# A third row block of attention probabilities is transposed through DRAM, with its spreads, PSUM banks and one reload moved

## What is computed

```python
qu, ku, vu, qc, kc, vc = split(xn @ W_qkv.T)            # each [b, 8 heads, 512, 64]
term1     = where(j > i, 0, qc*s @ vu.T)
lookahead = where(j > i, sigmoid(qu*s @ ku.T), 0)
Su        = term1 @ lookahead.T                          # [b, h, 512, 512]
scores    = qc*s @ kc.T - silu(Su);  masked where j > i
out       = softmax(scores) @ vc
ffn       = (silu(xn @ wg.T) * (xn @ wu.T)) @ wd.T       # hidden size 768, int weights / 127
```

## Time and profile before

| what | value |
|---|---|
| median of 3 runs | 1081.72 us (1080.22 to 1082.07) |
| the profiled execution | 1082.21 us, its span 1080.2 us |
| TensorE busy | 1058.2 us, 98% of the span |
| VectorE busy | 871.9 us, 81% |
| ScalarE busy | 755.8 us, 70% |
| GpSimd busy | 567.1 us, 52% |
| TensorE's granted clock, mean | 0.996 |

### The profile page before, as it was taken

One profiled execution on the slowest core, in us unless ns is written; L12 is line 12 of the kernel. 1 busy time (PEld: TensorE's weight loads), 2 busy tenths in 40 slices (PEclk: granted clock), 3 DMA queues, 4 the chain that ended last, 5 costly groups with the idle time before them and its releaser, 6 DMA issues.

```text
span 1080.2 us, 21562 instructions
## 1 busy us (share of the span) xinstructions
PE 1058.2 (98%) x7652; PEld 947.6 (88%) x7652; DVE 871.9 (81%) x1831; ACT 755.8 (70%) x1483; POOL 567.1 (52%) x630
## 2 busy tenths in 40 slices
PE   6999999999999999999999999999999899999998
PEld 5888888888888888888888889988889888899997
DVE  5788789888988898889888988888777768667766
ACT  6678777877787778777877787778777755443333
POOL 5355565556555655565556555656555545422230
PEclk9999999999999999999999999999999989999999
DMA  5032434343434343344334343433324546556631
GB/s 195 1 79 64 118 89 110 76 104 102 91 96 101 105 101 86 91 116 89 99 77 130 79 109 76 125 79 80 98 59 123 161 144 237 175 179 217 214 133 60
DMA packets 246076, 120.72 MB, mean 112 GB/s; under 512 B 161232, under 2 KB 227024, under 8 KB 243920
## 3 DMA queue, kind: packets, MB, share of 16 engines
q1 hardware_dynamic: 245968, 119.31, 40.5%
HBM read 64.75 MB, written 54.53 MB: 110 GB/s over the span
## 4 chain that ended last, share of the span: by engine, by line
PE 89%; DVE 3%; ACT 2%; issue 2%; POOL 1%; DMA 1%; SPq 1%; DVEq 0%; POOLq 0%; ACTq 0%
PE X L833 23%; PE X L748 20%; PE X L986 7%; PE X L885 7%; PE X L977 7%; PE X L817 6%; PE X L801 5%; PE X L787 5%; PE X L772 4%; PE X L867 4%; POOL prob L668 1%; DMA xT<-xT_copy 1%; DVE L_s L1457 1%; ACT prob L1176 1%; ACT T_s L1154 1%
## 5 line engine op out<-in xcount | busy, mean ns | idle before, releaser
L668 POOL TENSOR_SCALAR prob<-prob,inv 128x512 f32<-128x512 f32 (+3 forms) x256 | 301.4, 1194 | 16.3 <-DVE inv L1499 16.3
L833 PE MATMUL X<-L_s,T_s 128*128 128x128 f32 (+3 forms) x1920 | 281.7, 301 | 2.0 <-DVE L_s L1457 2.0
L833 PEld LDWEIGHTS X<-L_s,T_s 128*128 128x128 f32 x1920 | 267.5, 189 | 13.4 <-issue 2.8
L748 PE MATMUL X<-xT,W 128*128 128x512 f32 (+1 forms) x972 | 244.8, 399 | 0.0
L748 PEld LDWEIGHTS X<-xT,W 128*128 128x128 f32 x972 | 175.7, 191 | 40.8 <-issue 0.4
L1168 ACT ACTIVATE gate<-X 128x1024 f32<-128x1024 f32 (+1 forms) x96 | 84.9, 884 | 154.7 <-PE X L833 154.7
L642 POOL TENSOR_SCALAR_AFFINE_SELECT gate<-gate 128x256 f32<-128x256 f32 (+1 forms) x96 | 47.5, 495 | 205.2 <-DVE gate L1471 205.2
L1471 DVE SCALAR_TENSOR_TENSOR gate<-gate,X 128x1024 f32<-128x1024 f32 (+1 forms) x96 | 99.6, 1038 | 64.0 <-ACT gate L1168 64.0
L658 POOL TENSOR_SCALAR_AFFINE_SELECT T_s<-T_s 128x512 fp32r<-128x512 f32 x128 | 104.6, 829 | 85.4 <-DVE T_s L1464 85.4
L1176 ACT ACTIVATE prob<-prob,least 128x512 f32<-128x512 f32 (+3 forms) x256 | 141.8, 587 | 1.5 <-DVE least L1487 1.5
L1487 DVE CUSTOM_DVE_ANT_0 prob<-X,gate 128x512 f32<-128x512 f32 (+3 forms) x256 | 112.8, 487 | 25.8 <-PE X L817 24.2
(11 more groups left out here) (108 smaller groups left out, 1888.2 us busy)
## 6 DMA issues: line engine op xcount, KB each, us to landing
heads_out<-o_s SPq DMA_DIRECT2D x62, 256.0 KB, 3.3
prob_raw<-prob SPq DMA_DIRECT2D x240, 64.0 KB, 1.9
PT_s<-prob_raw SPq DMA_DIRECT2D x120, 128.0 KB, 2.4
xT_copy<-xT SPq DMA_DIRECT2D x8, 1024.0 KB, 6.8
w_split<-w_parts SPq DMA_DIRECT2D x22, 256.0 KB, 2.5
W<-w_split SPq DMA_DIRECT2D x12, 384.0 KB, 6.9
xT<-xT_copy SPq DMA_DIRECT2D x4, 1024.0 KB, 6.3
tanh_l<-in_L_attn_x SPq DMA_DIRECT2D x8, 512.0 KB, 4.9
```

The lines of the kernel that those rows point to most:

```text
L668: last = pool.tensor_scalar(v, v, inv[:, h, w - 1:w], None, ALU.mult)
L748: last = pe.matmul(out[:, tokens], sh.W[:, a, k, cols], xT[:, c, k, tokens], start=(n == 0), stop=(n == 3 * KD - 1))
L833: last = pe.matmul(both[:, h, at:at + (J + 1) * P], T_s[:, h, a, to:to + P], L_s[:, h, c, WIDE[J + 1]:WIDE[J + 1] + (J + 1) * P], start=(J ...
```

## The change

- Query row block 2 (query rows 256 to 383, three blocks per head) leaves TensorE too. `turn_heads` now transposes three blocks per head, both heads in one go, behind `sum_up` 0; `high_heads` and `low_heads` copy them in two instructions each. Nothing is transposed behind `sum_up` 1.
- `row_in_squares` runs twice on VectorE: row block 3 (128x1024) and, behind low VU, row block 2 (128x768). `prob` is laid out by row block, so that both heads lie side by side and a row block leaves in 4 spreads instead of 8.
- SyncE issues the 4 spreads of row 3 and the 4 of row 2, and only then the loads of row 3 (4) and row 2 (3).
- `high_rows` and `low_rows` work on 128x1536 and 128x256 elements, where `high_last_row` and `low_last_row` worked on 128x768 and 128x256.
- VectorE's low QU and low KU move behind `inverse` 2.
- Banks: `sum_up` 0 goes to banks 2 and 3, `sum_up` 1 to 6 and 7 (they swap), and the products of the last steps follow.
- `load_xT(0)` moves from step 31 to step 30, behind `load_gate_up` and ahead of the spreads; `load_down_out` stays in step 31, with no wait of its own.

The diff, cut to its core:

```diff
-         ("Su", 0, (6, 7)), ("PH", 0, (0, 1)), ("PT", 0, (0, 1)), ("PT", 1, (4,)), ("Su", 1, (2, 3)),
-         ("PH", 1, (6, 7)), ("PT", 2, (6, 7)), ("Su", 2, (4, 5))]
+         ("Su", 0, (2, 3)), ("PH", 0, (0, 1)), ("PT", 0, (0, 1)), ("PT", 1, (4,)), ("Su", 1, (6, 7)),
+          ("PT", 2, (2, 3)), ("Su", 2, (4, 5))]
...
+        def prob_row(h, w):
+            return flat_prob[:, 2 * WIDE[w] + h * w * P:2 * WIDE[w] + (h + 1) * w * P]
...
                 if part == LAST and q == 3:
+                    load_down_out()
+                if part == LAST and q == 2:
+                    load_gate_up()
                     sp.wait_ge(proj_filled, proj_count(LAST_G, KC))
                     sp.wait_ge(v_filled, LAST_G + 1)
                     sp.wait_ge(xT_stored, BATCH * 16)
                     load_xT(0)
-                    load_down_out()
-                if part == LAST and q == 2:
-                    load_gate_up()
                 if back1 and g - 1 < SQUARED:
-                    spread_last_row(g - 1, back2)
+                    for I in (3, 2):
+                        spread_row(g - 1, I)
+                    if back2:
+                        sp.wait_ge(o_filled, 2 * g - 2)
+                    for I in (3, 2):
+                        gather_row(g - 1, I)
...
+            def spread_row(g, I):
+
+                sp.wait_ge(row_in_squares_done[I], g + 1)
+                sp.sem_inc(ticks, 1)
+                to = prob_raw[I][g].rearrange("h q r t -> r (h q) t")
+                for i in range(4):
+                    sp.dma_start(to[:, :, i * 32:(i + 1) * 32],
+                                 prob_rows(I + 1)[i * 32:(i + 1) * 32, :].rearrange("r (q t) -> r q t", t=32)) \
+                      .then_inc(row_spread[I], 16)
+
+            def gather_row(g, I):
+
+                raw = prob_raw[I][g]
+                sp.wait_ge(row_spread[I], (g + 1) * 4 * 16)
+                for K in range(I + 1):
+                    sp.dma_start(PT_blocks[:, :, LOW, WIDE[TT - K] // P + I - K, :],
+                                 raw[:, 4 * K:4 * K + 4, :, :].rearrange("h q r t -> (q r) h t")) \
+                      .then_inc(row_loaded[I], 16)
...
+            def turn_heads(part, b, g):
+
+                pe.wait_ge(prob_ready, after(g - 1, 2))
+                tile = take_bank(part, b, g, "PH", 0)
+                for h in range(2):
+                    for i, (K, I) in enumerate([(0, 0), (0, 1), (1, 1)]):
+                        last = pe.transpose(tile[:, h, i * P:(i + 1) * P],
+                                            prob_row(h, I + 1)[:, K * P:(K + 1) * P], ident[:, :])
                 last.then_inc(PT_filled, 1)
...
+            def high_rows(g):
+
+                for I in (3, 2):
+                    act.wait_ge(row_loaded[I], (g + 1) * (I + 1) * 16)
+                act.activation(three_pairs(HIGH).bitcast(F32R), three_pairs(LOW), ACT.Copy).then_inc(rows_high, 1)
+                act.activation(PT_blocks[:, :, HIGH, 7, :].bitcast(F32R), PT_blocks[:, :, LOW, 7, :], ACT.Copy) \
+                   .then_inc(rows_high, 1)
...
                 if j == 0 and not (isinstance(g, int) and g == 0):
                     wait_before(dve, PT_filled, turned(g - 1, 1 if g - 1 < SQUARED else 2))
                     if g - 1 < SQUARED:
-                        wait_before(dve, last_row_spread, g * 8 * 16)
+                        wait_before(dve, row_spread[3], g * 4 * 16)
+                if j == 1 and 0 <= g - 1 < SQUARED:
+                    wait_before(dve, row_spread[2], g * 4 * 16)
...
+            def row_in_squares(g, I):
+
+                dve.wait_ge(prob_ready, after(g, 3 - I))
+                dve.transpose(prob_rows(I + 1), prob_rows(I + 1)).then_inc(row_in_squares_done[I], 1)
+
+            def low_rows(g):
+
+                dve.wait_ge(rows_high, 2 * g + 1)
+                dve.tensor_tensor(three_pairs(LOW).bitcast(F32R), three_pairs(LOW), three_pairs(HIGH), ALU.subtract) \
+                   .then_inc(rows_low, 1)
+                dve.wait_ge(rows_high, 2 * g + 2)
+                dve.tensor_tensor(PT_blocks[:, :, LOW, 7, :].bitcast(F32R), PT_blocks[:, :, LOW, 7, :],
+                                  PT_blocks[:, :, HIGH, 7, :], ALU.subtract).then_inc(rows_low, 1)
...
                 if back1:
                     inverse(g - 1, 2)
+                if ahead:
+                    low_proj(g + 1, QU, par)
+                    low_proj(g + 1, KU, par)
                 if back1 and g - 1 < SQUARED:
-                    row_in_squares(g - 1)
+                    row_in_squares(g - 1, 3)
                 if ahead:
                     low_proj(g + 1, VU, par)
+                if back1 and g - 1 < SQUARED:
+                    row_in_squares(g - 1, 2)
```

More of the change, by code:

```diff
@@ L311, in layer @@
         prob_ready = sem("prob_ready")
[L312 to L316, removed]
+        row_in_squares_done = {I: sem(f"row{I}_in_squares") for I in (3, 2)}
+        row_spread = {I: sem(f"row{I}_spread") for I in (3, 2)}
+        row_loaded = {I: sem(f"row{I}_loaded") for I in (3, 2)}
+        rows_high = sem("rows_high")
+        rows_low = sem("rows_low")
         PT_high = sem("PT_high")
@@ L928, in step @@
                 if back1 and g - 1 < SQUARED:
-                    turn_head(part, b, g, 0)
+                    turn_heads(part, b, g)
                 elif back1:
@@ L933, in step @@
                 sum_up(part, b, g, 1)
-                if back1 and g - 1 < SQUARED:
-                    turn_head(part, b, g, 1)
-                elif back1:
+                if back1 and g - 1 >= SQUARED:
                     turn_probs(part, b, g, 2)
@@ L1341, in step @@
                 if back2 and g - 2 < SQUARED:
-                    high_last_row(g - 2)
+                    high_rows(g - 2)
                 high_L(g, 0)
@@ L1372, in step @@
                 if back1 and g - 1 < SQUARED:
-                    high_head(g - 1, 0)
+                    high_heads(g - 1)
                 elif back1:
@@ L1377, in step @@
                 gate_of(g, 1)
-                if back1 and g - 1 < SQUARED:
-                    high_head(g - 1, 1)
-                elif back1:
+                if back1 and g - 1 >= SQUARED:
                     high_PT(g - 1, 2)
@@ L1512, in low_PT @@
                 dve.tensor_tensor(out, src, high.bitcast(F32), ALU.subtract).then_inc(PT_low, 1)
-            def low_head(g, h):
-                dve.wait_ge(PT_high, turned(g, h))
-                src = bank("PH", h)
-                for at, part in ((0, lambda a: PT_blocks[:, h, a, 0:8, :].rearrange("p (n i) c -> p n (i c)", n=2)[:, :, 0:2 * P]),
-                                 (2 * P, lambda a: PT_blocks[:, h, a, 2:9:6, :])):
-                    n = 2 * P if at == 0 else P
-                    last = dve.tensor_tensor(part(LOW).bitcast(F32R), src[:, :, at:at + n], part(HIGH), ALU.subtract)
-                last.then_inc(PT_low, 1)
@@ L1524, in row_in_squares, with low_heads @@
-            def row_in_squares(g):
-                dve.wait_ge(prob_ready, after(g, 0))
-                dve.transpose(prob[:, :, 0:SEQ], prob[:, :, 0:SEQ]).then_inc(last_row_in_squares, 1)
-            def low_last_row(g):
-                for i, at in enumerate((slice(3, 10, 3), slice(7, 8))):
-                    dve.wait_ge(last_row_high, 2 * g + i + 1)
-                    dve.tensor_tensor(PT_blocks[:, :, LOW, at, :].bitcast(F32R), PT_blocks[:, :, LOW, at, :],
-                                      PT_blocks[:, :, HIGH, at, :], ALU.subtract).then_inc(last_row_low, 1)
+            def low_heads(g):
+                dve.wait_ge(PT_high, turned(g, 0))
+                src = bank("PH", 0)
+                dve.tensor_tensor(PT_s[:, :, LOW, 0:2 * P], src[:, :, 0:2 * P], PT_plain[:, :, HIGH, 0:2 * P], ALU.subtract)
+                dve.tensor_tensor(PT_blocks[:, :, LOW, 4, :].bitcast(F32R), src[:, :, 2 * P:3 * P],
+                                  PT_blocks[:, :, HIGH, 4, :], ALU.subtract).then_inc(PT_low, 1)
@@ L1707, in step @@
                 if back2 and g - 2 < SQUARED:
-                    low_last_row(g - 2)
+                    low_rows(g - 2)
                 if g == 0:
@@ L1790, in build @@
     xT_raw = [nc.dram_tensor(f"xT_raw{b}", [TT, 8, 32, P], F32).ap() for b in range(BATCH)]
-    prob_raw = [nc.dram_tensor(f"prob_raw{g}", [2, 16, 32, P], F32).ap() for g in range(SQUARED)]
+    prob_raw = {I: [nc.dram_tensor(f"prob_raw{I}_{g}", [2, 4 * I + 4, 32, P], F32).ap() for g in range(SQUARED)] for I in (3, 2)}
     heads_out = nc.dram_tensor("heads_out", [2, BATCH * INNER, SEQ], F32).ap()
```

71 lines of the change are left out of this document (24 added, 47 removed).

## The result

| | us | runs |
|---|---|---|
| before, median | 1081.62 (1077.11 to 1082.64) | 14 |
| changed, median | 1084.52 (1081.44 to 1085.21) | 14 |
| ratio, 95% interval | 1.0031 [1.0020, 1.0041] | |
| changed, profiled execution | 1081.44, its span 1079.6 | 1 |

The change makes the kernel 0.3% slower, where the prediction had 1077.4 us and "faster". The range held the time, the sign was wrong. The profiled execution is the fastest of its 14; how the two traces stand to the two medians is told further down.

The account below looks back on a forecast made before the run. TensorE's own work, 98% of the span, was the bound. Steps other than q = 1 -6.7, q = 1 steps +5.5, step 1 +0.3, step 31 -3.9: -4.8 us from 1082.21 to 1077.4; 8-in-10 range 1069 to 1089.

Parts of the forecast that it names:

- second term: `low_rows` ahead of `attend`: ends at 515.35, giving TensorE a new stall of 0.31 us in each step from 2 on.
- sign of being wrong: The forecast is wrong if `low_rows` takes under 2.1 or over 2.6 us, L867 always waits, or `high_rows` awaits a DMA.
- The quiet length: `low_rows` on VectorE with GpSimd idle: 1536 + 256 elements take 2.09 us.
- The slowing: Extra time of `low_rows` beside GpSimd's norm: 0.27 us, as the norm lies beside it for the same 1.26 us.
- `attend` waits longer: Rival, slower: stall s at L885 decides from 0.52 us; at 0.64 us it gives 1085.0 us; chance 0.17.
- the bound of 0.64: Upper bound of the stall at `attend`: twice the slowing for twice the length, `low_rows` at 2.69 us.
- the cover holds: Rival, faster: VectorE's signal comes before TensorE's need at `attend`, stall 0.03 us, 1071.0 us; chance 0.16.
- the q = 1 steps: Steps 5, 9, ... 25: low QC 1.51 us later, transposes 0.60 shorter, each step 0.91 us longer, +5.5 for six.
- The wait of the transposes: At L867, for low QC: 1.2 to 1.6 us, in q = 1 steps only.
- The spare of 0.3 us for low QC: In q = 0, 2, 3: low QC's signal at 524.29 against transposes at 524.60, so its delay is hidden.
- step 31's term: x loaded in step 30 ends TensorE's wait and half clock; VectorE becomes the limit: -3.9 us, bounds 0 and -5.3.
- the clock falls in the waits of q = 1: Rival, slower: TensorE's clock falls in waits of 1.4 us, six times 1.7 us, 1087.6 us; chance 0.03.

Follow-up runs that it names:

- e6: Changed kernel with GpSimd's mask of tanh 2 ahead of its norm 0, all work kept: 1078.15 us, ratio to before 0.9976.
- e4: Changed kernel with VectorE's low QC ahead of row 2's squares and of x's scaling: 1077.91 us, ratio to before 0.9978.
- e5: Changed kernel with GpSimd's norm of query rows 384 to 511 cut to 16 columns of each head: 1077.32 us, ratio to before 0.9961.
- e1: The changed kernel run again, unedited, beside the kernel before: 1084.39 us against 1080.18, ratio 1.0033.
- e3: Kernel before with only x's reload moved to step 30: 1077.32 us, ratio to before 0.9966.
- e7: Changed kernel with TensorE's scores 2 between the projections QU and KU: 1078.46 us, ratio to before 0.9978.
- e8: Changed kernel with the edits of e4 and e6 together: 1068.37 us, ratio to before 0.9880.
- e10: e8 with scores 2 between the projections QU and KU, as in e7: 1071.68 us, ratio to before 0.9910.
- e2: Changed kernel with x's reload put back into step 31: 1089.75 us, ratio to before 1.0085.

## Why the prediction was wrong

**The step that failed is the size of `low_rows`**, its second term. It had 2.36 us; the trace has 2.70 us, more than the 2.6 that the prediction named as its sign of being wrong (groups by shape, mean of 30):

```profile
L1545 DVE TENSOR_TENSOR PT_s<-PT_s 128x1536 fp32r<-128x1536 f32 x30 | 64.0, 2134 | 0.0
...
L1548 DVE TENSOR_TENSOR PT_s<-PT_s 128x256 fp32r<-128x256 f32 x30 | 18.6, 619 | 0.0
```

The quiet length was right (2.09; 2.10 in step 31 and in e6). The slowing was 0.60 us and not 0.27. I had held it fixed because the norm's end is fixed, as if the slowing were a share of the time spent side by side. It is a wait for whoever started first. The old pair started 0.31 us behind the norm's second half (512.68; 512.99 in the earlier trace rows) and lost 0.24 us; the new one starts 0.16 us behind it and loses 0.39, so in both it went on some 0.55 us behind the norm's start. The length of an operation has no part in that. Step 3 of e4 has the new length at the old distance (GpSimd, then VectorE):

```profile
102.02 3.12 POOL L685 TENSOR_SCALAR prob<-prob,inv 128x512 f32<-128x512 f32 x2
```
```profile
103.87 1.99 DVE L1545 TENSOR_TENSOR PT_s<-PT_s 128x1536 fp32r<-128x1536 f32 x1
```

The second half starts near 102.02 + 3.12 - 1.57 = 103.57, `low_rows` 0.30 us behind it, and its first instruction loses 1.99 - 1.75 = 0.24 us, just what the old pair lost. The second loss, of 0.2 us, fell on the 256-element operation, behind a mask that I had not priced: it runs into `low_rows` only because `low_rows` is longer. Both together made the stall 0.58 us, past the 0.52 from which I had the rival "`attend` waits longer" decide, inside the bound of 0.64. With s = 0.58 the prediction's own sum is 23 x (0.58 - 0.60) + 1.9 = +1.4, or 1083.6 us: that rival, near its middle. The rival "the cover holds" was mis-sized too. It had 1071 us for a stall of 0.03, and e5, with no stall, takes 1077.3: the 0.3 us that low QC has to spare hang on the stall of 0.31, and that sum left them as they were.

The Trainium skill (SBUF — State Buffer, Who interferes with whom) says of the shared ports that issue order decides who blocks. The trace agrees in step 31 and in e6, where GpSimd's operation stood still behind VectorE's; the prediction read the page's rule as refuted. (The page says "the whole instruction" of VectorE's two-port modes, which it says `tensor_tensor` does not have.) In the other direction it holds in part: VectorE waited until some 0.55 us behind the start of an operation of 1.57 us, not for the whole of it.

**What held.** Transposes -0.60 us each, `high_rows` 1.52 us, row 2's squares 0.88 us from start to start (498.29 to 499.17 in step 17) for 0.87, the q = 1 steps +0.9 us (forecast 0.91), step 31 -4.0 us (from its start to `sum_up` 0: 856.03 to 877.49 before, 860.54 to 877.99 now; forecast -3.9). The wait of the transposes was said to be in q = 1 steps only, and is; it reads 0.95 us, not 1.2 to 1.6, since the later `attend` hides part of it. In step 1, where no `low_rows` delays it, it is 2.0. No DMA is waited for in the steps; the eight spreads took SyncE 4.77 us to issue (526.10, step 18) where the prediction had 7.2, a term that was mis-sized but hidden either way. The spare of 0.3 us for low QC in the other steps was right too: e6 moved `attend` by 0.58 us and found 0.23 of it taken there.

**Medians and traces.** By the traces the change gives -0.8 us, by the medians +2.9. Two things lie between them. The changed kernel's profiled execution had a short tail: its last store is issued 0.9 us later than before's and its span ends 3.8 us behind that, where before has 5.3 and e1 5.7. And the profiled execution of before had the whole loss of step 31, while the median of its runs has less of it (e3: 2.9 us). The changed kernel takes 0.6 us more in step 31 than e3, from its start to `sum_up` 0 (17.45 and 872.02 - 855.20 = 16.82), so of the 2.9 some 2.3 are left for step 31's term, and the steps add up to 23 x -0.02 + 5.5 + 0.3 - 2.3 = +3.0 us, at the +2.9 and under the +4.2 measured beside e1. This is an estimate: it takes e3's gain between medians for what the changed kernel gains.

A third thing may lie there. In the changed kernel's two traces the wait of 2.05 us in step 1 has the full clock behind it. In e5, e6 and e7 the same wait is followed by a stretch at the lower level. TensorE in step 1 of e7, then the busy times of each engine, the granted clock (0.52) and the DMAs from 63 to 66 us:

```profile
62.78 1.23 PE L884 MATMUL X<-ident,prob 128*128 128x128 f32 x6 [2.06 <-DVE qc_s L1434]
63.66 5.99 PE L850 MATMUL X<-L_s,T_s 128*128 128x384 f32 x36
```
```profile
63.00:66.00 3.00, 3.00 (x16) 3.00 (x14) 3.00 (x4) 0.87 (x2) 0.00 (x0) 0.52 0.75 116
```

The same 36 matmuls have a length of 4.68 us in the changed kernel's trace, and from the transposes' start to the look-ahead behind scores 0 it is 7.6 us in e7 and 6.0 there: 1.6 us. The prediction's rival "the clock falls in the waits of q = 1" is borne out in step 1 of three traces, but in none of the waits of 1.4 to 1.6 us in the later q = 1 steps. In how many of the changed kernel's executions the clock falls there is not known. What sets its fall in one execution and not in another stays open, here and in the kernel before.

## What to carry over

When an operation grows on an engine that signals the bottleneck, price it by who starts first at each neighbour, not by a share of overlap: that error, 2.36 us for an instruction pair of 2.70, decided the sign of the whole change. Work freed on the bottleneck comes back as the first wait in line, and behind it stands the next one; here two repairs brought 6.5 and 6.2 us alone and 16.0 together (e8). And hold a combination against the old kernel with the same side edits: 5.4 us (1080.98 - 1075.55) of the 12.7 between e8 and before are x's load and low QC's place, which need no moved row.

## What was new about the hardware

- VectorE's two-input operation and GpSimd's norm take turns by who starts first. Behind VectorE, a 128x512 norm of 1.57 us took 3.2 (4.76 - 1.57 in e6) and ended some 1.35 us behind the second of VectorE's two instructions, whether it had started 0.2 or 0.65 us behind the first (e6, e10); behind the norm, VectorE lost 0.39 us when it started 0.16 us behind, and 0.24 us at 0.30, at either length; a 128x256 mask went from 0.42 to 1.06 us. Why the norm lets VectorE in after some 0.55 us, no run shows.
- A stretch of 36 matmuls took TensorE 0.34 us longer in an order with two more changes between products over 64 and over 128 rows, with no wait recorded (e8, e10).
- One and the same wait can leave TensorE's clock alone or not: behind 2.05 us in step 1 the changed kernel's trace has the upper level of 2.4 GHz, behind 2.06 us e7's has 0.52 granted over 3 us, near the lower level of 1.2 GHz. Behind 1.6 us (e5, e6) the clock stayed up; behind 3.89 us in e2 eight matmuls took 3.78 us, as at the lower level in the earlier trace rows.
